# An adapter and routed-expert kernel: four buffers for x's parts, an own stack for tile 0, another warm-up operand, and a split weight load

## The reference

```python
h   = x @ W.T + b + 2.0 * (x @ lora_A[slot]) @ lora_B[slot]       # cond, per batch
out = x + h @ base_w.T + base_b
        + 0.5 * sum_e combine[e] * (h @ A.T) @ B[e].T             # ffn
# combine: softmax(h @ router_w.T), top 2 of 16, divided by their sum
```

## Time and profile before

| | us |
|---|---|
| runs of the kernel before | 104.66, 103.49, 103.99; median 103.99 |
| the profiled execution's own time | 103.44 |
| its span, first to last instruction | 101.6 |
| time outside the span | 1.84 |
| PE busy | 97.4 (96% of the span) |
| DVE, ACT, POOL busy | 65.1, 39.8, 18.7 |

### The profile page before, as it was taken

One profiled execution on the slowest core, in us unless ns is written; L12 is line 12 of the kernel. 1 busy time (PEld: TensorE's weight loads), 2 busy tenths in 40 slices (PEclk: granted clock), 3 DMA queues, 4 the chain that ended last, 5 costly groups with the idle time before them and its releaser, 6 DMA issues.

```text
span 101.6 us, 1806 instructions
## 1 busy us (share of the span) xinstructions
PE 97.4 (96%) x576; PEld 88.1 (87%) x576; DVE 65.1 (64%) x182; ACT 39.8 (39%) x97; POOL 18.7 (18%) x34
## 2 busy tenths in 40 slices
PE   5899999999999999999999999999999999999990
PEld 5799999999989999988988997899788788888990
DVE  2529999948567867959946735677368726656101
ACT  3404446885519726554435126120920604031000
POOL 5100003000397990070330061000000000000000
PEclk9999999999999999999999999999999999999999
DMA  2999789999854172592672280470065191940311
GB/s 42 321 318 377 225 182 372 340 424 422 230 96 68 26 216 58 168 267 68 182 254 59 79 231 1 117 205 6 14 165 165 20 266 46 239 170 0 110 52 52
DMA packets 8089, 16.91 MB, mean 166 GB/s; under 512 B 1475, under 2 KB 3907, under 8 KB 7952
## 3 DMA queue, kind: packets, MB, share of 16 engines
q1 hardware_dynamic: 7472, 16.40, 53.5%
q10 hardware_dynamic: 576, 0.39, 1.2%
q0 software_dynamic: 32, 0.00, 0.0%
HBM read 13.28 MB, written 2.16 MB: 152 GB/s over the span
## 4 chain that ended last, share of the span: by engine, by line
PE 71%; issue 11%; POOL 11%; DMA 3%; ACT 1%; DVE 0%; POOLq 0%
PE pair L771 69%; POOL x_lo L352 4%; POOL e_lo L370 4%; DMA w_raw_all<-w_cat 3%; POOL p_lo L364 2%; POOL p_hi L362 1%; PE pair L919 1%; PE pair L921 1%; ACT p_hi L418 1%; PE pair L939 1%; ACT w_hi_all L392 0%; DVE xn L765 0%; POOLq L361 0%
## 5 line engine op out<-in xcount | busy, mean ns | idle before, releaser
L771 PE MATMUL pair<-e_hi,w_hi_all 128*128 128x512 f32 (+1 forms) x72 | 27.2, 378 | 0.0
L771 PE MATMUL pair<-e_lo,w_hi_all 128*128 128x512 f32 (+1 forms) x72 | 26.7, 370 | 0.0
L771 PE MATMUL pair<-e_hi,w_lo_all 128*128 128x512 f32 (+1 forms) x72 | 26.6, 370 | 0.0
L771 PE MATMUL pair<-p_hi,x_hi 128*128 128x304 f32 x64 | 19.7, 308 | 0.2 <-POOL p_lo L364 0.2
L771 PE MATMUL pair<-p_lo,x_hi 128*128 128x304 f32 x64 | 19.4, 302 | 0.0
L771 PE MATMUL pair<-p_hi,x_lo 128*128 128x304 f32 x64 | 19.3, 302 | 0.0
L771 PEld LDWEIGHTS pair<-e_hi,w_lo_all 128*128 128x128 f32 x72 | 13.6, 188 | 2.6
L771 PEld LDWEIGHTS pair<-e_hi,w_hi_all 128*128 128x128 f32 x72 | 13.6, 188 | 2.4
L771 PEld LDWEIGHTS pair<-e_lo,w_hi_all 128*128 128x128 f32 x72 | 13.6, 189 | 1.8
L712 DVE TENSOR_TENSOR exp_raw_all<-w_raw_all 128x512 f32<-128x512 f32 x16 | 10.4, 689 | 7.5 <-DMA w_raw_all<-spill 7.5
L502 ACT ACTIVATE w_hi_all<-exp_raw_all 128x512 fp32r<-128x512 f32 x16 | 9.6, 627 | 13.8 <-DVE exp_raw_all L712 13.8
(11 more groups left out here) (107 smaller groups left out, 131.5 us busy)
## 6 DMA issues: line engine op xcount, KB each, us to landing
w_raw_all<-spill SPq DMA_DIRECT2D x16, 256.0 KB, 3.9
exp_raw_all<-experts SPq DMA_DIRECT2D x4, 512.0 KB, 8.7
xn<-x_n SPq DMA_DIRECT2D x4, 512.0 KB, 7.3
out<-xn SPq DMA_DIRECT2D x7, 256.0 KB, 4.0
w_raw_all<-w_cat SPq DMA_DIRECT2D x3, 552.0 KB, 6.8
xt_raw<-x_t SPq DMA_DIRECT2D x2, 512.0 KB, 6.3
xt_raw<-x_t SPq DMA_DIRECT2D x1, 1024.0 KB, 12.6
c_stack<-c_hi SPq DMA_DIRECT2D x7, 74.0 KB, 4.2
```

What stands on the lines that cost most here:

```text
L771: return nc.tensor.matmul(out_ap, lhs, rhs, start=first, stop=last)
```

## The change

**Warm-up.** `WARM_UP` is 13. The operand is `idle`, a view of the program's own constant 0.0, one float32 per partition read 256 times over (`nc.const_aps.tensor(0.0, (P, 2 * P), F32)`). Its type is F32, where `zeros` was F32R. The constant is written by POOL ahead of the block, so `warm` and `pe_warm` go, and with them DVE's memset of `e_hi`.

**Weights.** Block 1 comes as two transfers: SP loads its second-layer columns, ACT its W columns as a third transfer. ACT makes the high part of the first half of block 0's W in two pieces of 128 columns, and the folds wait for each piece. The small loads b1 and b2 move behind the adapter tables.

**x's parts.** Four buffers instead of two: those of t % 4 = 2 and 3 lie in blocks 2 and 3 of `w_hi` and `w_lo`, whose W columns are free once the folds are done. ACT makes x_hi(2) and x_hi(3) right after the folded parts, POOL their low parts early, and `lora_a_parts(t)` goes ahead of `x_lo_part(t)` from tile 4 on.

**Tile 0's stack.** `c_first` is `c_stack[:, 0]`, of 98 rows: c_hi in rows 0 to 15 (ACT copy) and 32 to 47 (DVE copy), c_lo in rows 64 to 79 (DVE copy), bias rows in 96 and 97, zeros between. h's high and low parts are made before the transpose, so that one transpose and one pair of matmuls replace the transpose and four pairs. DVE clears three tiles for it at the start.

**Bias and experts.** `bias_part` starts from `b2_rows`, one instruction fewer. ACT splits the experts' quarters later, c_hi goes ahead of bp_hi, and the wait for POOL's low parts moves into the experts' product of tile 0.

```diff
-WARM_UP = 11
+WARM_UP = 13
...
-        zeros = e_hi[:, 0, 0:2 * P]
+
+        idle = nc.const_aps.tensor(0.0, (P, 2 * P), F32)
...
-            for k in range(1, KC):
+
+            sp.dma_start(w_raw[:, 1, D:], w_cat[1, :, D:]).then_inc(in_w2_next, 16)
+            for k in range(2, KC):
                 load_w(k)
...
+            act.dma_start(w_raw[:, 1, 0:D], w_cat[1, :, 0:D]).then_inc(in_w[1], 16)
             act.wait_ge(in_w_side[0], 16)
-            nc.scalar.activation(w_hi[:, 0, W_LEFT], w_raw[:, 0, W_LEFT], ACT.Copy).then_inc(wh_left, 1)
+            for cols in (slice(0, P), slice(P, 2 * P)):
+                nc.scalar.activation(w_hi[:, 0, cols], w_raw[:, 0, cols], ACT.Copy).then_inc(wh_left, 1)
...
             x_lo_part(2)
+            x_lo_part(3)
             lora_a_parts(2)
             split_experts_lo(2)
-            x_lo_part(3)
             lora_a_parts(3)
             split_experts_lo(3)
             for t in range(4, NT):
+                lora_a_parts(t)
                 x_lo_part(t)
-                lora_a_parts(t)
...
-            act.wait_ge(pe_warm, 1)
+            act.wait_ge(in_xt[1], 16)
+            x_hi_part(2)
+            x_hi_part(3)
             split_experts(0)
-            split_experts(1)
-            act.wait_ge(bias_step, KC + 1)
-            nc.scalar.activation(bp_hi[:, :], bias_part[:, :], ACT.Copy).then_inc(bph_done, 1)
             act.wait_ge(pe_c, 1)
             nc.scalar.activation(c_hi[:, :], w2_cols(ps_c), ACT.Copy).then_inc(ch_done, 1)
+            act.wait_ge(bias_step, KC)
+            nc.scalar.activation(bp_hi[:, :], bias_part[:, :], ACT.Copy).then_inc(bph_done, 1)
+            act.wait_ge(first_set, 2)
+            act.wait_ge(ch_done, 1)
+            nc.scalar.activation(c_first[0:R, :], c_hi[0:R, :], ACT.Copy).then_inc(first_high, 1)
...
-            nc.vector.memset(zeros.bitcast(F32), 0.0).then_inc(warm, 1)
+            nc.vector.memset(b2_rows[:, :], 0.0).then_inc(first_set, 1)
+            nc.vector.memset(c_first.bitcast(F32), 0.0).then_inc(first_set, 1)
+            nc.vector.memset(h_first[:, :], 0.0).then_inc(first_set, 1)
...
+            lora_first_lo()
+            dve.wait_ge(first_set, 2)
+            nc.vector.tensor_copy(c_first[F_AGAIN:F_AGAIN + R, :], c_hi[0:R, :]).then_inc(first_high, 1)
+            dve.wait_ge(cl_done, 1)
+            nc.vector.tensor_copy(c_first[F_LOW:F_LOW + R, :], c_lo[0:R, :]).then_inc(first_low, 1)
             split_experts_lo(0)
-            lora_first_lo()
             stack_bias()
...
-            pe.wait_ge(warm, 1)
             for _ in range(WARM_UP):
-                last = mm(ps_warm, zeros[:, 0:P], zeros, True, True)
-            last.then_inc(pe_warm, 1)
+                mm(ps_warm, idle[:, 0:P], idle, True, True)
...
                 pe.wait_ge(ht_done, 1)
-                pe.wait_ge(ch_done, 1)
-                part(ht_first_hi[:, :], c_hi, False)
-                pe.wait_ge(cl_done, 1)
-                part(ht_first_hi[:, :], c_lo, False)
-                pe.wait_ge(ht_first_done, 1)
-                part(ht_first_lo[:, :], c_hi, False)
+                pe.wait_ge(first_high, 2)
+                pe.wait_ge(first_low, 1)
                 pe.wait_ge(bias_rows, 1)
-                part(ones[HR:HT, :], c_stack[HR:HT, 1, :], True).then_inc(pe_z, 1)
+                nc.tensor.matmul(ps_z[0][:, z_small[0]:BANK], ht_first[:, :], c_first[:, 0:border],
+                                 start=False, stop=True, skip_group_check=True)
+                nc.tensor.matmul(ps_z[0][:, BANK:BANK + W2N - border], ht_first[:, :], c_first[:, border:],
+                                 start=False, stop=True, skip_group_check=True).then_inc(pe_z, 1)
```

More of the change, by code:

```diff
@@ L47 @@
 T_H = P - 2 * R
+F_AGAIN, F_LOW, F_BIAS = 32, 64, 96
+FT = F_BIAS + 2
 NB = 3
+XB = 4
 FOLDS = (1, 0, 2, 3)
@@ L120, in adaln_ffn_kernel, with x_split @@
         rden = sb("rden", [P, 1])
+        def x_split(split, w_split):
+            return [split[:, b] for b in range(2)] + [
+                w_split[:, b, 0:D].rearrange("p (k n) -> p k n", k=KC) for b in range(2, XB)]
+        x_his, x_los = x_split(x_hi, w_hi), x_split(x_lo, w_lo)
         weight_rows = w_raw_all[:, 0:NB * GC * P].rearrange("p (a j n) -> p a j n", a=NB, j=GC)
@@ L141, in adaln_ffn_kernel @@
         ps_ht = pairs[3][0:2 * R, 0:P]
-        ps_ht_first = pairs[3][:, 0:P]
+        ps_ht_first = pairs[3][0:FT, 0:P]
         ps_rt = pairs[3][:, P:2 * P]
@@ L346, in _ @@
             pool.memset(probs[:, E:E + 8], -1.0).then_inc(consts, 1)
-            pool.memset(h_first[:, :], 0.0).then_inc(consts, 1)
             def x_lo_part(t):
-                par = t % 2
                 pool.wait_ge(xh_done, t + 1)
-                pool.tensor_tensor(x_lo[:, par].rearrange("p k n -> p (k n)"), xt_raw[:, t, :],
-                                   x_hi[:, par].rearrange("p k n -> p (k n)").bitcast(F32),
+                if t < XB:
+                    pool.wait_ge(pe_p, KC)
+                pool.tensor_tensor(x_los[t % XB], xt_raw[:, t, :].rearrange("p (k n) -> p k n", k=KC),
+                                   x_his[t % XB].bitcast(F32),
                                    ALU.subtract).then_inc(x_done, 1)
@@ L440, in lora_first @@
                 act.wait_ge(pe_first, 1)
[L441 to L443 removed]
+                act.wait_ge(first_set, 6)
+                src = ps_z[0][:, z:z + R].unsqueeze(1).to_broadcast([P, 2, R])
+                nc.scalar.activation(h_first[:, :].rearrange("p (a n) -> p a n", a=2)[:, :, 0:R].bitcast(F32R), src,
+                                     ACT.Copy, scale=LORA_SCALE).then_inc(hh_done, 1)
             def lora_first_t():
                 act.wait_ge(pe_ht, 1)
[L447 removed]
+                nc.scalar.activation(ht_first[:, :], ps_ht_first, ACT.Copy).then_inc(ht_done, 1)
             def lora_hi(t):
@@ L615, in _ @@
             x_lo_early(1)
+            bias_part_of(0)
             dve.wait_ge(lbh_done, 1)
@@ L859, in x_side @@
                         pe.wait_ge(pl_done, KC)
-                    for n, (lhs, rhs) in enumerate(((x_hi, p_hi), (x_hi, p_lo), (x_lo, p_hi))):
-                        last = mm(ps_z[par][:, out_cols], lhs[:, par, k, :], rhs[:, k, cols],
+                    for n, (lhs, rhs) in enumerate(((x_h, p_hi), (x_h, p_lo), (x_l, p_hi))):
+                        last = mm(ps_z[par][:, out_cols], lhs[:, k, :], rhs[:, k, cols],
                                   k == 0 and n == 0, k == KC - 1 and n == 2)
```

144 lines of the change are left out of this document (67 added, 77 removed).

## The result

The change made the kernel slower. Its median is 107.92 us (107.42 to 108.6), that of the kernel before on the same chip 103.72 us (103.49 to 104.66), five runs each: ratio 1.0394 [1.0326, 1.0462]. The profiled execution took 108.33 us with a span of 106.5. Its partner of before, 103.44, lies just under that kernel's five runs, so the two profiles differ by 4.9 us and the medians by 4.2.

The account below looks back on a forecast made before the run. It took PE's queue, behind 4.24 us, to bound the kernel: 103.44 + 4.2 (warm-up) - 1.0 (tile 0's product) - 0.2 (POOL's p_lo) = 106.4 us, range 105.0 to 107.9.

Parts of the forecast that it names:

- The warm-up: Start of PE: 13 float32 products at four passes each delay the folds and C, + 4.2 us.
- The first two rivals: Warm-up: a float32 product costs one pass, 101.9 us, chance 0.13; or two passes, 103.4 us, chance 0.06.
- The third: Warm-up: float32 products in pieces do not raise the clock, 112.0 us, chance 0.05.
- Where PE begins: Start: PE, needing no memset, begins at 0.87 us instead of 1.20.
- Tile 0's product: Two matmuls replace eight, gaining 1.10 us less 0.1 of waiting for bias rows; term - 1.0 us.
- 0.7 us of room: Tile 0's stack: h_first and DVE's low part finish by 24.1 us, before the transpose at 24.83.
- 0.4 of room: Tile 0's stack: DVE's two copies end near 25.1 us, before x_first(1) at 25.48.
- The bounds for the stack: Tile 0: added work on ACT and DVE costs PE between 0 and + 0.5 us.
- POOL's p_lo: x_first(4): with x's parts of tiles 2 and 3 made early, POOL is no longer late; - 0.2 us.
- experts' quarters … hidden: Quarters 1 to 3, split one step later, are needed some 15 us on, so the delay is hidden.
- The split load: Start: split load and pieces of W worth nothing under the long warm-up, at most 0.2 us without it.
- The fourth rival: The forecast with the stack's waits lost as well: 106.9 us, inside the range; no separate chance given.

Follow-up runs that it names:

- e2: The kernel before with only the 13 float32 warm-up products on the constant, no memset: 107.10 us, ratio 1.0284.
- e3: The change with three float32 warm-up products instead of 13: 105.17 us, ratio 1.0107.
- e5: The change with its warm-up constant read as F32R, POOL's x_lo behind DVE's bias rows and its experts' quarters later: 103.84 us, ratio 0.9979.
- e9: The change with F32R warm-up constant, POOL's x_lo and experts' quarters held back for DVE, and block 1 loaded whole: 103.12 us, ratio 0.9876.
- e10: The change with only block 1 loaded whole by SyncE, float32 warm-up kept: 108.26 us, ratio 1.0354.
- e7: The change with its warm-up constant read as F32R and block 1 loaded whole by SyncE: 104.52 us, ratio 1.0054.
- e1: The change with one edit, its warm-up constant read as F32R: 105.46 us, ratio 1.0117.
- e4: The change with POOL's x_lo parts held until DVE's last bias_part and its experts' quarters until DVE's second: 107.61 us, ratio 1.0311.

## Why the prediction was right, and where it was not

**The warm-up: right, and the reason too.** Predicted: 26 entries, 0.91 us a product, first fold at 9.2, C at 22.4, + 4.2 us. In the profile: 26 entries, first fold at 8.99, C at 22.28, + 4.07. e2 shows that it is this edit, e3 measures its price at the lower level as 0.90 us. At the higher level a product took 0.44 instead of 0.47, which is most of the 0.2 us by which the first fold came early. The Trainium skill's page "FP8 and Floating Point Precision", TensorE Precision Notes, gives four passes to true FP32; e3's 0.90 against 4 x 0.222 = 0.89 agrees. One sum in that passage is written wrong: 576 - 6 + 2 + 2 + 13 is 587, and the 585 of the page are 576 - 8 + 2 + 2 + 13. Nothing hangs on it. The first two rivals (one pass, two passes) fall by that. The third, a clock that does not rise, falls by the 404 ns of the later entries.

**Where PE begins: 0.78 instead of 0.87.** Without weight.

**Tile 0's product: the mechanism right, the net wrong.** "Term: - 1.0 us" was + 0.08 in the profiles (lag 4.07 at C, 4.15 behind the product). The gross gain is there, 1.02 instead of 1.10. The step that failed is "0.7 us of room" and "0.4 of room": the working took DVE's and ACT's instructions at the durations that they had in the trace of before, moved by their places in the order, and left out what POOL would be doing meanwhile. With x_lo of tiles 2 and 3 made early, POOL ran from 23.74 to 26.82, just where DVE has its bias_part, and the room was gone. The bounds for the stack, 0 and + 0.5, were too narrow: it was 1.10, of which the sum had 0.1 as the wait for the bias rows. About 0.9 of it goes without POOL beside DVE (in e5 and e9 0.2 are left).

**POOL's p_lo: right in its place, wrong in its net.** The wait at x_first(4) is gone, and gave back 0.44 where the term had 0.2. But the "experts' quarters … hidden" of the same paragraph fails: the quarter that POOL does later coincides with DVE's, which cost 1.26 us at x_first(3). Nobody waited for POOL's part; they waited for DVE, whose e_lo it held up, and POOL was there because ACT's split of that quarter had been put later.

**The split load: right for the change, wrong in what is under the cover.** At nothing, with the warm-up as the cover: e10 shows it. "With it gone they are worth up to … 0.2 us": with the warm-up gone the split is a loss, 1.0% from e9 to e5 and 0.6% from e7 to e1. Only the shorter conversion was counted, and not that the piece on the other queue lands later. The page "DMA: Bandwidth & Descriptors" of the Trainium skill, under Issuing engines are not separate DMA queues, says that SyncE's and ScalarE's transfers share the same engines; the rows agree in that the second queue brought nothing: 7.2 us for the needed piece against 5.8 to 6.1 for the whole block.

**The sum.** 103.44 + 4.07 from the warm-up, + 0.08 at tile 0, + 1.26 at x_first(3), - 0.44 at x_first(4), and about - 0.1 elsewhere are the 108.33 of the profile. The forecast was 106.4: the sign, the mechanism and its size were right, and the two gains of 1.2 us set against it did not arrive. So the median lies 1.5 us above the forecast, at the range's upper edge (107.9). The fourth rival, the stack's waits lost as well, comes nearest, but its 106.9 has no loss at x_first(3), and no sentence of the prediction has one. That the range reaches so far is owed to the 1.2 us given to the spread of the runs, so its upper edge held by luck; and the upper terms it names, 1.2 and 0.5, would add up to 108.1. That the loss by the medians (4.2) is less than by the profiles (4.9) comes from the profile of before, which is 0.3 under its own median, and the change's, which is 0.4 above; which part of the chain varies from run to run is not settled.

## What to carry to other kernels

A matmul on a plain float32 operand cost four times one of F32R here, though it only warmed the array up: look at the number of entries in the compiled order, and cast constants. When a change moves work of GpSimd, or of the engine whose results it waits for, list which DVE instructions with two SBUF inputs, and which of its copies between places in SBUF, run in the new window, and price each at the rest of POOL's instruction plus its own; a room read off the old trace holds only while the neighbours stay. And test a gain without the loss that covers it: here the split load looked free only because PE came 4 us late.

## What was not expected of the hardware

- The exclusion between DVE and POOL works in both directions and holds for tiny instructions as well: POOL's cast of 64 columns went from 0.24 to 1.24 us behind DVE's e_lo, and a copy of DVE of 592 columns with a single SBUF input from 0.46 to 1.35 (e4), so the list of what collides is longer than that of instructions with two inputs.
- The clock rises while four-pass products run (from 647 to 404 ns an entry in the changed kernel). The page's clock row shows the top digit from the first slice on, while entries took 647 ns and then 404: for the level at the start of this program it could not be relied on, and the distances between starts were.
- The moment of the rise differs between kernels with the same start: in e1 the pairs at 4.52 and 4.78 us lie 0.13 apart a matmul, while e7's two pairs at 4.85 and 5.35 are still 0.25 apart a matmul. What decides it was not found. The last pair of block 0 began at 7.48 in e1 and at 8.05 in e7, so it moves what comes next by half a microsecond.
- A smaller load on a second queue (256 KB, 7.2 us) can land later than the larger one beside it (296 KB, 4.8 us), and later than both in one transfer (5.8 to 6.1 us).
